# Convolution pieces, row-transform copies and transposes in another order in the tail of a four-layer kernel

## The chip, the cores and the metric

The program runs on one core of one Trainium2 chip. The metric is the device time of one execution in microseconds (us), lower is better. A core has engines with instruction queues of their own that run side by side and meet only at semaphores: TensorE (PE) multiplies matrices into the banks of PSUM (tile `ps`), VectorE (DVE), ScalarE (ACT) and GpSimd (POOL) do elementwise work, and SyncE (SP) starts transfers. Each queue is worked off in order, so an instruction that waits holds up all that stand behind it.

## What is computed

Eight images of 32 channels and 128 x 128 pixels go through four layers, each with a group normalisation ahead of it and a residual sum behind it:

```python
x = x + _L0_conv_ref(_gn(x), ...)   # 3x3 convolution, batch norm, relu, spectral curvature
x = x + _L1_conv_ref(_gn(x), ...)   # per-pixel 9x9 operator made of channel norms, then a mix
x = x + _L2_conv_ref(_gn(x), ...)   # gate made of the image's edges
x = x + _L3_conv_ref(_gn(x), ...)   # product of a spectral branch and a 3x3 convolution
return x
```

The change lies in the stage that computes layer 2 and the first part of layer 3. In the reference these are

```python
# layer 2
x_gray = jnp.mean(x, axis=1, keepdims=True)
dog = _conv(x_gray, gk1, pad) - _conv(x_gray, gk2, pad)
gx, gy = _conv(dog, sobel_x, 1), _conv(dog, sobel_y, 1)
mag = jnp.sqrt(gx * gx + gy * gy + 1e-06)
att = jax.nn.sigmoid(mag * gate_w[0] + gate_b[0])
return x * (1.0 + ALPHA * att)
# layer 3
g = _global_transform(c, w1, w2)    # rfft2, 16 x 16 modes mixed over channels, irfft2
l = _local_transform(c, conv_w, conv_b)   # 3x3 convolution with wrapped borders
return g * l
```

## The kernel before

The program has four stages, one after the other: layer 0's convolution over all images, the spectral part of layer 0 with the norms for layer 1, layer 1's operator (the longest), and the **tail**, in which layers 2 and 3 run as a pipeline over the images. Behind the tail come the mixing of the spectra for all images at once (`mix_spectrum`, L867), the last image's convolution, and a loop that transforms back, multiplies and stores.

The tail is written out by hand, with no scheduler: each engine has a loop over the period `t` (on DVE `i`), and the order of the calls in it is the order in its queue. Image rows lie on the partitions. In period `t` three images are under way:

- Image `t+1` in layer 2: ACT normalises it in 4 quarters of 8 channels (`normalise(gn2, ...)`, L936) into the tile `xn3[(t+1) % 2]`. PE sums its channels to a grey picture in four quarters (`gray_sum`, L811), then filters it (`blur` L772, `sobel` L778 and L780). ACT copies between these steps and makes the gate's factor in `mag_root` and `att_tanh` (L1106, L1114); DVE finishes it in `magnitude` and `attention` (L1529, L1534).
- Image `t` on its way from layer 2 to layer 3: DVE multiplies by the gate and adds (`attend`, L1516 and L1519), and takes the statistics for the next normalisation gn3 (L1226). PE forms the means and variances over partitions (`group_means` L574, `group_vars` L581), with DVE's `group_deviations`, `group_shift` (L1246) and `group_scale` (L1251, L1253) and ACT's `group_root` (L930) between them. ACT normalises with gn3 in four quarters. PE makes the row transforms (`dft_rows`, four per image, L789, in banks 6 and 7 in turn), ACT copies each of them out (`dft_out`, L1066), and PE makes the column transforms (`dft_columns`, L801). DVE transposes the normalised image into the layout of the convolution (`bands`, L1542 to L1544), and POOL adds the halo rows (L1215, L1216).
- Images `t-1` and `t-2` in the 3x3 convolution (`conv3`, L591): each image has two halves of nine taps, cut into three pieces of three taps. Half 0 of image `t-1` runs between the row transforms, half 1 of image `t-2` between the grey sums. ACT empties the banks 0 to 3 after each half (`conv3_out`, L1080).

Beside that POOL and DVE prepare image `t+2`: POOL adds layer 1's output (`tail_sum`, L1202), DVE takes its statistics for gn2, and the gn2 mean, variance and scale go through the same PE and DVE steps as those of gn3.

The waits that the prediction walks along are these. The row transform `n` waits for the copy `n-2` (same bank). The column transforms wait for all four copies. ACT's normalisation of image `t+1` waits for `gn2.ready` of that image, set by `group_scale`, and for the transposes of image `t-1`, since both images use the same tile:

```python
after(act, bands_ready, t)
after(act, dfth_mm, 4 * t)
for q in range(4):
    normalise(gn2, t + 1, q, xn3[(t + 1) % 2], xd[(t + 1) % 3])
```

The transposes wait for all gn3 normalisations of their image. `conv3` waits before its first tap until the banks are emptied; the pieces of half 1 need nothing new after that.

## Time and profile before

| | us |
|---|---|
| median of 3 runs | 3924.25 |
| lowest, highest | 3917.05, 3925.5 |
| the profiled execution's own time | 3922.26 |
| its span in the profile | 3920.1 |
| tail, about | 3185 to 3640 |
| mixing of the spectra | 3640 to 3717 |
| back transforms and output | 3745 to 3920 |

Engine busy time over the whole span: PE 3338.9 us (85%), DVE 2855.7 (73%), ACT 1849.5 (47%), POOL 2341.5 (60%). These shares come from layer 1's operator above all. A reader should look at the tail alone: the table by stretch gives each engine's busy time in it, and the timelines give the start and the busy time of each group of instructions, with the idle time ahead of it and what ended that in brackets. A wait in brackets that is marked "issue" is one for which the profile shows no releaser.

### The profile page before, as it was taken

The page shows a single profiled execution, that of the slowest core. Times are in us where ns is not written, and L with a number is a line of the kernel's source. Part 1 is how long each engine was busy: PE and PEld are TensorE (multiplying, and loading weights), DVE is VectorE, ACT ScalarE, POOL GpSimd, SP SyncE. Part 2 cuts the span into 40 slices and gives each one's busy share as a digit, 9 for nine tenths or more (in the row PEclk, how much of TensorE's full clock was granted, in tenths as well). Part 3 has the DMA queues.
Part 4 walks back from the last instruction along what each step waited for, and adds up shares of the span by engine and source line. Part 5 has one row for each costly group of instructions (what it writes and reads, how often), then busy time and mean ns, then how long its engine had stood idle before and what let it go on. Part 6 is the DMA issues. An engine that isn't in the chain of part 4 may idle for free.

```text
span 3920.1 us, 89862 instructions
## 1 busy us (share of the span) xinstructions
PE 3338.9 (85%) x32900; PEld 1184.0 (30%) x32900; DVE 2855.7 (73%) x3513; ACT 1849.5 (47%) x2702; POOL 2341.5 (60%) x1131
## 2 busy tenths in 40 slices
PE   4678999759999999999999999999999957787565
PEld 2343444312212212222222222222222245555454
DVE  3652544469989989989989989989999956655034
ACT  0114566355545545555555555555555455665011
POOL 0000000049999999999999999999999923321000
PEclk9899999879999999999999999999999967888665
DMA  6574898566656656666666666666666664535589
GB/s 158 120 167 99 164 196 169 124 164 155 154 133 148 153 139 145 158 141 144 150 149 143 145 152 147 141 149 151 141 149 159 141 152 118 154 101 128 140 191 251
DMA packets 495204, 586.47 MB, mean 150 GB/s; under 512 B 71970, under 2 KB 334754, under 8 KB 489435
## 3 DMA queue, kind: packets, MB, share of 16 engines
q1 hardware_dynamic: 484212, 563.65, 62.5%
q10 hardware_dynamic: 10560, 16.93, 1.8%
q8 instruction: 287, 4.70, 0.5%
q14 instruction: 145, 1.19, 0.1%
HBM read 409.91 MB, written 184.54 MB: 152 GB/s over the span
## 4 chain that ended last, share of the span: by engine, by line
PE 30%; POOL 29%; issue 28%; DVE 5%; ACT 4%; DMA 2%; SPq 1%; ACTq 0%; POOLq 0%; DVEq 0%
POOL arena L1183 27%; PE ps L591 8%; PE ps L632 7%; PE ps L639 4%; PE ps L703 3%; POOL arena L1171 2%; ACT arena L936 2%; PE ps L789 1%; PE ps L811 1%; DVE arena L1542 1%; PE ps L685 1%; PE ps L898 1%; PE ps L867 1%; DMA arena<-x_dram 1%; DMA w_conv<-in_conv_w 1%
## 5 line engine op out<-in xcount | busy, mean ns | idle before, releaser
L1183 POOL TENSOR_TENSOR arena<-arena 128x1024 f32<-128x1024 f32 x896 | 1931.0, 2196 | 556.2 <-ACT arena L1039 556.2
L1494 DVE TENSOR_TENSOR arena<-ps,arena 128x1024 f32<-128x1024 f32 x1792 | 2107.4, 1220 | 204.9 <-PE ps L685 174.3
L703 PE MATMUL ps<-arena,w_mix 128*32 128x512 f32 x10752 | 1438.5, 607 | 79.4 <-POOL arena L1183 79.4
L1039 ACT ACTIVATE arena<-ps 128x1024 f32<-128x1024 f32 x896 | 918.9, 1026 | 1026.3 <-PE ps L695 1015.3
L685 PE MATMUL ps<-arena,sel 48*128 48x512 bf16 x3584 | 702.5, 385 | 24.8 <-issue 16.1
L685 PEld LDWEIGHTS ps<-arena,sel 48*128 48x128 bf16 x3584 | 190.1, 93 | 945.5 <-issue 936.8
L591 PE MATMUL ps<-arena,w_conv 32*32 32x512 f32 x9216 | 354.0, 650 | 42.6 <-issue 34.3
L695 PE MATMUL ps<-norms,opw 57*128 57x512 bf16 x1792 | 348.1, 384 | 49.2 <-ACT arena L971 17.5
L703 PEld LDWEIGHTS ps<-arena,w_mix 128*32 128x32 f32 x10752 | 214.3, 108 | 467.5 <-issue 467.5
L936 ACT ACTIVATE arena<-arena,nmr,rstd 128x128 f32<-128x128 f32 x768 | 300.5, 481 | 33.0 <-DVE arena L1544 30.4
L632 PE MATMUL ps<-arena,circ 128*128 128x512 f32 x640 | 287.9, 595 | 14.1 <-ACT arena L950 14.1
L695 PEld LDWEIGHTS ps<-norms,opw 57*128 57x128 bf16 x1792 | 101.8, 93 | 435.3 <-issue 430.0
L591 PEld LDWEIGHTS ps<-arena,w_conv 32*32 32x32 f32 x9216 | 179.1, 107 | 178.8 <-issue 125.5
L1215 POOL COPY arena<-arena 32x130 f32<-32x130 f32 x32 | 33.8, 1057 | 327.7 <-DVE arena L1544 326.7
L1166 POOL TENSOR_TENSOR arena<-arena 128x1024 f32<-128x1024 f32 x62 | 133.0, 2145 | 95.7 <-ACT arena L980 95.7
L1580 DVE TENSOR_TENSOR arena<-arena,ps 128x512 f32<-128x512 f32 x64 | 43.7, 683 | 192.7 <-PE ps L898 163.3
L639 PE MATMUL ps<-arena,circ 128*128 128x512 f32 x384 | 176.3, 594 | 0.0
L632 PEld LDWEIGHTS ps<-arena,circ 128*128 128x128 f32 x640 | 120.3, 189 | 166.6 <-issue 166.6
L1226 DVE BATCH_NORM_STATS2 st<-arena 128x6 f32<-128x128 f32 x768 | 156.5, 278 | 7.1 <-POOL arena L1202 4.9
L1422 DVE TENSOR_TENSOR arena<-arena 128x512 f32<-128x512 f32 x64 | 44.3, 692 | 143.1 <-ACT arena L955 141.1
L1159 POOL TENSOR_TENSOR col<-col,powers 128x1 f32<-128x1 f32 x8 | 4.4, 549 | 241.1 <-DVE col L1282 241.1
L811 PE MATMUL ps<-arena,ident 128*128 128x128 f32 x512 | 78.8, 319 | 70.0 <-ACT arena L936 69.9
(151 smaller groups left out, 2195.2 us busy)
## 6 DMA issues: line engine op xcount, KB each, us to landing
arena<-pad SPq DMA_DIRECT2D x768, 260.0 KB, 7.7
split_dram<-arena SPq DMA_DIRECT2D x64, 768.0 KB, 3.6
arena<-split_dram SPq DMA_DIRECT2D x1536, 32.0 KB, 3.2
x_dram<-arena SPq DMA_DIRECT2D x16, 2048.0 KB, 7.8
l_dram<-arena SPq DMA_DIRECT2D x128, 256.0 KB, 4.2
arena<-l_dram SPq DMA_DIRECT2D x32, 1024.0 KB, 14.1
arena<-x_dram SPq DMA_DIRECT2D x16, 2048.0 KB, 16.4
pad<-arena SPq DMA_DIRECT2D x8, 2080.0 KB, 16.4
```

What stands on the lines that cost most here:

```text
L591: m = pe.matmul(ps[C * j:C * j + C, bank + g, :], weights[C * g:C * g + C, dy, dx, :], tile[C * g:C * g + C, r:r + CR, dx:dx + W], start=t ...
L632: m = pe.matmul(ps[:, n % 2, :], circ[:, d, :], yp[h % 2][:, 4 * n:4 * n + 4, 4 - d:4 - d + W], start=d == 0, stop=d == 4)
L639: m = pe.matmul(ps[:, 2 + n % 2, :], circ[:, 5 + d, :], yp[h % 2][:, 4 * n:4 * n + 4, 4 - d:4 - d + W], start=d == 0, stop=d == 2)
L685: m = pe.matmul(ps[:, 2 * (n % 2) + e, :], sel[ROWS2 * e:ROWS2 * e + SPLIT_ROWS, u % GROUP, :], split[ROWS2 * e:ROWS2 * e + SPLIT_ROWS, pa ...
L695: m = pe.matmul(ps[:, POOL_BANK + e, :], opw[ROWS2 * e:ROWS2 * e + KROWS, SPREAD[c], :], norms[ROWS2 * e:ROWS2 * e + KROWS, buf, half, :]. ...
L703: m = pe.matmul(ps[C * g:C * g + C, SUM + chunk % 2, :], w_mix[:, s, :], ring[:, (first + g // 2) % size, NPX * (g % 2):NPX * (g % 2) + NP ...
L936: m = nc.scalar.activation(tile[:, c, :], src[:, c, :], ACT.Identity, scale=rstd[:, gn.slot + n % 2, c:c + 1], bias=nmr[:, gn.slot + n % 2 ...
L1039: nc.scalar.activation(ring_p[:, slot, :], ps[:, POOL_BANK:POOL_BANK + 2, :].rearrange("p a n -> p (a n)"), ACT.Tanh).then_inc(tanh_p, 1)
L1166: nc.gpsimd.tensor_tensor(rest, tt, hml[:, 0, :], ALU.subtract).then_inc(rows_r, 1)
L1183: nc.gpsimd.tensor_tensor(slot, slot, pixels(chunk % 2, SPREAD[n // 2], n % 2), ALU.mult).then_inc(prod_p, 1)
L1226: m = nc.vector.bn_stats(st[:, c, :], tile[:, c, :])
L1494: nc.vector.tensor_tensor(slot, weights, pixels(par, ONCE[n // 2], n % 2), ALU.mult).then_inc(prod_d, 1)
```

## The change

In PE's loop of the tail the three pieces of the convolution's half 1 are placed otherwise: the first at the end of the period before, behind `dft_columns`, the second ahead of the first grey sum, the third ahead of the second grey sum. In ACT's loop each copy of a row transform comes one place later: copy 0 behind the third gn3 quarter, copy 1 behind the fourth, copy 2 behind the tanh. In DVE's loop `bands` goes ahead of `attention` and of `group_scale` of gn2. Nothing is added or removed; all loops of other stages are as before.

```diff
--- before.py
+++ after.py
@@ -827,10 +827,10 @@
             TAP_PARTS = ((0, 1, 2), (3, 4, 5), (6, 7, 8))
             for t in range(-2, B + 1):
                 for n in range(4):
+                    if t >= 2 and n < 2:
+                        conv3(t - 2, 1, TAP_PARTS[n + 1])
                     if 0 <= t + 1 < B:
                         gray_sum(t + 1, n)
-                    if t >= 2 and n < 3:
-                        conv3(t - 2, 1, TAP_PARTS[n])
                 if 0 <= t < B:
                     after(pe, dftw_copy, 3 * t)
                     group_means(gn3, t)
@@ -854,6 +854,8 @@
                     if t + 2 < B:
                         pe.wait_ge(gn2.shifted, t + 3)
                     dft_columns(t)
+                if 1 <= t < B:
+                    conv3(t - 1, 1, TAP_PARTS[0])
 
             def mix_spectrum():
 
@@ -1107,11 +1109,13 @@
                 for q in range(4):
                     if 0 <= t < B:
                         normalise(gn3, t, q, xn3[t % 2], xd[t % 3])
-                        if q:
-                            dft_out(t, q - 1)
+                        if q >= 2:
+                            dft_out(t, q - 2)
                 if 0 <= t + 1 < B:
                     act.wait_ge(mag_root, t + 2)
                     nc.scalar.activation(r2[:, :], rn[:, :], ACT.Tanh, scale=gate_h[:, 0:1], bias=gate_h[:, 1:2]).then_inc(att_tanh, 1)
+                if 0 <= t < B:
+                    dft_out(t, 2)
                 if t + 2 < B:
                     group_root(gn2, t + 2)
                 if 0 <= t < B:
@@ -1559,12 +1563,12 @@
                     tail_stats(i + 2)
                     group_deviations(gn2, i + 2, t)
                     group_shift(gn2, i + 2)
+                if i >= 0:
+                    bands(i)
                 if 0 < i + 1 < B:
                     attention(i + 1)
                 if i + 2 < B:
                     group_scale(gn2, i + 2, t)
-                if i >= 0:
-                    bands(i)
 
             for b in range(B):
                 x3, l3 = xe[b % 3], le[b % 3]
```

On PE, from the column transforms at the end of one period to the Sobel filter of the next; the rows of before:

```order
L801 MATMUL ps<-k,arena 32x32 x64
L811 MATMUL ps<-arena,ident 128x128 x8
L591 MATMUL ps<-arena,w_conv 32x512 x48
L811 MATMUL ps<-arena,ident 128x128 x8
L591 MATMUL ps<-arena,w_conv 32x512 x48
L811 MATMUL ps<-arena,ident 128x128 x8
L591 MATMUL ps<-arena,w_conv 32x512 x48
L811 MATMUL ps<-arena,ident 128x128 x8
L574 MATMUL ps<-st,k 128x32 x2
L772 MATMUL ps<-gray,k 128x128 x5
```

and the same place in the changed kernel:

```order
L801 MATMUL ps<-k,arena 32x32 x64
L591 MATMUL ps<-arena,w_conv 32x512 x96
L811 MATMUL ps<-arena,ident 128x128 x8
L591 MATMUL ps<-arena,w_conv 32x512 x48
L811 MATMUL ps<-arena,ident 128x128 x24
L574 MATMUL ps<-st,k 128x32 x2
L772 MATMUL ps<-gray,k 128x128 x5
```

Two pieces (96 matmuls) now stand between the column transforms and the first grey sum, one behind that sum, and the last three sums follow each other. (One matmul of the program shows as two in the profile's counts.)

On ACT, from the gn3 normalisations to the end of the period; before:

```order
L936 ACTIVATE arena<-arena,nmr,rstd 128x128 x16
L1066 COPY arena<-ps 128x512
L936 ACTIVATE arena<-arena,nmr,rstd 128x128 x8
L1066 COPY arena<-ps 128x512
L936 ACTIVATE arena<-arena,nmr,rstd 128x128 x8
L1066 COPY arena<-ps 128x512
L1114 ACT_TABLE_LOAD
L1114 ACTIVATE r<-rn,gate_h 128x128
L930 ACT_TABLE_LOAD
L930 ACTIVATE root<-sd 128x32
L1066 COPY arena<-ps 128x512
```

and in the changed kernel, whose line numbers are 2 higher here:

```order
L938 ACTIVATE arena<-arena,nmr,rstd 128x128 x24
L1068 COPY arena<-ps 128x512
L938 ACTIVATE arena<-arena,nmr,rstd 128x128 x8
L1068 COPY arena<-ps 128x512
L1116 ACT_TABLE_LOAD
L1116 ACTIVATE r<-rn,gate_h 128x128
L1068 COPY arena<-ps 128x512
L932 ACT_TABLE_LOAD
L932 ACTIVATE root<-sd 128x32
L1068 COPY arena<-ps 128x512
```

Three copies moved back by one place each; the two table loads stay.

On DVE, from `group_shift` to `attend`; before:

```order
L1246 TENSOR_SCALAR sd<-ps 128x32
L1534 TENSOR_SCALAR ra<-r 128x128
L1251 RECIPROCAL rstd<-root 128x32
L1253 SCALAR_TENSOR_TENSOR nmr<-mu,rstd 128x32
L1542 STREAM_TRANSPOSE arena<-arena 128x128x32
L1543 STREAM_TRANSPOSE arena<-arena 128x32
L1544 STREAM_TRANSPOSE arena<-arena 128x32
L1516 TENSOR_TENSOR arena<-arena,ra 128x1024 x4
```

and in the changed kernel, whose line numbers are 4 higher here:

```order
L1250 TENSOR_SCALAR sd<-ps 128x32
L1546 STREAM_TRANSPOSE arena<-arena 128x128x32
L1547 STREAM_TRANSPOSE arena<-arena 128x32
L1548 STREAM_TRANSPOSE arena<-arena 128x32
L1538 TENSOR_SCALAR ra<-r 128x128
L1255 RECIPROCAL rstd<-root 128x32
L1257 SCALAR_TENSOR_TENSOR nmr<-mu,rstd 128x32
L1520 TENSOR_TENSOR arena<-arena,ra 128x1024 x4
```

The three transposes moved ahead of the three small instructions, and stay behind `group_shift`.

## Rows read from the trace of the kernel before

**Rows 1.** Table by stretch: busy us (instructions) of each engine, PEclk, DMA share, GB/s.

```profile
3353.60:3414.60 61.00, 46.05 (x868) 31.40 (x868) 34.07 (x96) 36.40 (x85) 18.75 (x12) 0.86 0.52 140
3474.20:3531.70 57.50, 44.57 (x868) 31.17 (x868) 34.10 (x96) 36.40 (x85) 18.75 (x12) 0.86 0.25 75
```

**Rows 2.** Timeline of PE, period 5: start, busy us, instructions [idle before <- what ended it].

```profile
3477.43 3.78 PE L811 MATMUL ps<-arena,ident 128*128 128x128 f32 x16 [9.25 <-ACT arena L936]
...
3485.01 2.05 PE L811 MATMUL ps<-arena,ident 128*128 128x128 f32 x16
3486.99 3.41 PE L591 MATMUL ps<-arena,w_conv 32*32 32x512 f32 x96
...
3497.53 0.54 PE L574 MATMUL ps<-st,k 128*128 128x32 f32 x4
...
3523.58 2.12 PE L801 MATMUL ps<-k,arena 128*32 128x32 f32 x128 [1.89 <-issue]
```

**Rows 3.** Timeline of ACT, period 5.

```profile
3474.20 12.44 ACT L936 ACTIVATE arena<-arena,nmr,rstd 128x128 f32<-128x128 f32 x32 [5.07 <-DVE arena L1544]
3497.73 0.27 ACT L1092 COPY gray<-ps 128x128 f32<-128x128 f32 x1 [11.10 <-PE ps L811]
...
3503.28 6.26 ACT L936 ACTIVATE arena<-arena,nmr,rstd 128x128 f32<-128x128 f32 x16
3509.43 0.57 ACT L1066 COPY arena<-ps 128x512 f32<-128x512 f32 x1
...
3514.29 3.19 ACT L936 ACTIVATE arena<-arena,nmr,rstd 128x128 f32<-128x128 f32 x8
...
3523.38 2.13 ACT L1080 ACTIVATE arena<-ps,bias 128x1024 f32<-128x1024 f32 x2
...
3531.75 4.72 ACT L936 ACTIVATE arena<-arena,nmr,rstd 128x128 f32<-128x128 f32 x12 [5.11 <-DVE arena L1544]
```

**Rows 4.** Timeline of DVE, one row of period 1, then period 5.

```profile
3258.91 2.50 DVE L1235 TENSOR_TENSOR dev<-st,mu 128x32 f32<-128x32 f32 x2
...
3474.06 4.87 DVE L1516 TENSOR_TENSOR arena<-arena,ra 128x1024 f32<-128x1024 f32 x4
...
3483.78 6.27 DVE L1226 BATCH_NORM_STATS2 st<-arena 128x6 f32<-128x128 f32 x32
...
3523.04 0.35 DVE L1251 RECIPROCAL rstd<-root 128x32 f32<-128x32 f32 x1 [0.99 <-ACT root L930]
...
3523.53 8.05 DVE L1542 STREAM_TRANSPOSE arena<-arena 128x4096 f32<-128x4096 f32 x1
```

**Rows 5.** Timeline of PE, the means of period 1 and the first sum of period 6.

```profile
3258.04 0.61 PE L574 MATMUL ps<-st,k 128*128 128x32 f32 x4 [1.43 <-issue]
...
3534.99 3.78 PE L811 MATMUL ps<-arena,ident 128*128 128x128 f32 x16 [9.29 <-ACT arena L936]
```

**Rows 6.** Table by stretch, PE alone: PE busy, PEclk, DMA share, GB/s.

```profile
3504.00:3506.00 2.00, 0.95 (x31) 1.00 0.93 248
3524.00:3526.00 2.00, 1.70 (x116) 0.50 0.04 8
3262.00:3264.00 2.00, 1.90 (x9) 0.50 0.47 104
```

**Rows 7.** Timelines of DVE and PE, end of period 6 and period 7.

```profile
3579.42 8.10 DVE L1542 STREAM_TRANSPOSE arena<-arena 128x4096 f32<-128x4096 f32 x1
...
3581.82 10.64 PE L591 MATMUL ps<-arena,w_conv 32*32 32x512 f32 x288
3603.65 1.04 PE L574 MATMUL ps<-st,k 128*128 128x32 f32 x4 [11.19 <-issue]
...
3606.95 5.58 PE L591 MATMUL ps<-arena,w_conv 32*32 32x512 f32 x96
```

**Rows 8.** Timeline of PE: a piece in period 3, and the mixing of spectra.

```profile
3397.84 2.17 PE L591 MATMUL ps<-arena,w_conv 32*32 32x512 f32 x43 [2.04 <-issue]
...
3657.78 2.05 PE L867 MATMUL ps<-cs,arena 32*32 32x16 f32 x128 [7.45 <-issue]
```

**Rows 9.** DMA issues, 3180 to 3640 us: line, KB each, median us to landing.

```profile
arena<-x_dram SPq DMA_DIRECT2D x5, 2048.0 KB, 8.4
```

## Prediction

> **What bounds the kernel now.** I read first the table by stretch, then the timelines of PE, ACT and DVE over one period of the tail. The tail runs from about 3185 to 3640 us of the 3920.1 us span; nothing ahead of it or behind it is touched, so only its periods count. I call a period's start the moment when ACT begins the 32 gn2 normalisations of the next image: 3295.6, 3353.6, 3414.6, 3474.2 and 3531.75 for periods 2 to 6. So periods 2 to 5, four of one pattern, take 58.0, 61.0, 59.6 and 57.5 us; two of them stand in [rows 1]. No engine is full there: PE has 44.6 to 46.2 us of busy time, DVE 34.1, ACT 36.4, POOL 18.75. The period is a ring of waits, and it must be walked.
>
> Period 5, from 3474.20. ACT is done with its 32 normalisations after 12.44 us, then stands 11.10 us for PE's grey sum [rows 3]. DVE multiplies, adds and takes statistics and is done at 3490.05, but PE's means, which it waits for, start at 3497.53 [rows 2, 4]. Both wait for the same queue: PE starts the first grey sum 3.2 us into the period, and runs four sums with three convolution pieces between them, until 3497.7, 23.5 us in. PE's grey sum, with the convolution inside it, is what comes last. Then come means, blur, variances and Sobel, and ACT starts the gn3 normalisations at 3503.28: **29.1 us** after the period's start. From there: four quarters with three copies between them, tanh and its table, the root and its table (which waits for DVE's `group_shift`, and that for PE's variances; I read it at 3521.72), `attention`, `group_scale`, and only then the transposes at 3523.53. The next period starts 8.22 us later, at 3531.75: **28.5 us** after the start of the gn3 normalisations [rows 2 to 4].
>
> **Part 1, the convolution pieces.** At the clock's high level a quarter of the grey sum costs 1.98 us from its start to the next one's (3485.01 to 3486.99) and a piece 3.34 (3.41 less the same 0.07 of overlap) [rows 2]. After the change two of the three pieces stand ahead of the first sum, one of them behind the column transforms of the period before. I need that PE has room there: the column transforms end at 3525.7, and the next sum starts at 3534.99 after 9.29 us idle [rows 2, 5]. Two pieces are 6.7 us, so they fit. The first needs ACT to have emptied the banks (L1080, done at 3525.5, ahead of PE anyway [rows 3]), so that new wait costs nothing. At high clock the sums then end: first sum 3.2 to 5.2 us into the period, one piece to 8.5, second sum 10.5, third 12.5, fourth 14.5 (ACT's last quarter is there at 12.45). So PE comes down from 23.5 to 14.5. But the means wait for DVE too, which starts `attend` at the period's start and takes 16.0 us (3474.06 to 3490.05) [rows 4]; in the new order it starts 0.16 us ahead of ACT, which puts the means at 15.9. **What is late next is DVE's `attend`**, not PE, and of the 9.0 us only about 7.6 come through. From means to the first gn3 normalisation is 5.75 us now (3497.53 to 3503.28), less 0.3 since ACT's L1080 is over by the time the blur ends: 5.45. That gives 21.4 us instead of 29.1.
>
> The clock. After its 9.29 us of idle time PE's first sum takes 3.78 us instead of 2.05: it runs at 0.50, the low level (1.2 GHz), which the engine has had since the column transforms [rows 2, 6]. In the new order PE works until about 0.6 us into the period and then waits 2.6 us for ACT's first quarter. The gap of 1.89 us ahead of the column transforms brought it down; in 3504 to 3506, with 1.05 us idle, it stayed at 1.00 [rows 2, 6]. So I count a low spell here as likely. It can cost the 1.7 us of one sum; the fourth sum then ends at 16.2, just by DVE's 15.9. I add 0.5 us per period for it. By the same rows the gap before the means (14.5 to 15.9) may take the clock down in the periods where the first didn't.
>
> **Part 2, transposes ahead of `attention` and `group_scale`; copies later.** Moving the copies shifts ACT, not PE. A normalised quarter is 3.1 us and a copy 0.5 [rows 3]. The first copy comes 9.9 us after the start instead of 6.7, and the third row transform, which needs it, starts at 13.75 behind PE's pieces: 3.9 us of slack. The second copy ends at 13.7, wanted at 15.7: 2.0 us of slack. The quarters end at 13.0 instead of 14.2 (3514.29 + 3.19). The transposes wait for all four and then for `group_shift`, which PE's variances let go 18.5 us after the start; they stay where they are. So the transposes start at 18.55 instead of 20.25: 1.7 us earlier [rows 4]. `attention` and `group_scale` now stand behind them, and ACT's next normalisation needs their result: 0.14 for `attention`, 0.49 from the reciprocal to what follows `group_scale` (3523.04 to 3523.53), in all about 0.65 us more than now [rows 4]. Net **1.1 us**: 27.4 instead of 28.5. A new steady period is 21.4 + 27.4 + 0.5 = **49.3**, say 49.5 us.
>
> **Part 3, period 6 and 7.** Period 6 has no image of gn2 left, so no `group_shift` holds the transposes: they start as soon as ACT's last quarter is done, 13.0 us after 3561.07 instead of 18.35 (3579.42) [rows 7]. `attend` of the last image, and with it PE's wait of 11.19 us for the means at 3603.65 [rows 7], follow: 37.4 us after the gn3 start instead of 42.6, **5.2 us**, on top of the 7.7 of the front half. PE's pieces lie in that wait. Period 7 keeps its time: PE at a clock of 0.50 and then its three pieces lead there, and the copies have slack. The mixing of spectra and the output stage only shift.
>
> **Code fetch.** PE's gaps marked "issue" in the mixing of spectra come after every 128 matmuls; the 16 of them are 1.4 to 7.45 us, the long ones while many loads run; in period 3 such a gap of 2.04 us, and in period 4 a slow piece, lie in the second half [rows 8], and they are the reason why those periods are 3.5 and 2.1 us longer than period 5. The new order issues column transforms and two pieces on end; the same with three pieces stands in period 7 and takes 10.64 instead of 10.0 us [rows 7], so little is lost. In the second half the instructions stand as densely as before. Ends: none of these stalls left (0), or 2.04 us in each of the four periods and those of before (about 14). I take 3, half of what periods 2 to 4 show over period 5 (0.5 + 3.5 + 2.1). The Trainium skill (Runtime: NRT & Kernel Launch, section Instruction fetch mechanics) says that the next block of code is fetched while this one runs and that crossing a block is mostly hidden. By that rule this term would be 0 and the forecast 3 us lower; the gaps of [rows 8] speak against it.
>
> **The sum.** Period 0: 0.25 us (transposes earlier by 0.9, 0.65 more behind them). Period 1: 1.1 us; it has no convolution in its front half and keeps its 25 us there, which hold a DVE stall of 2.2 us [rows 4]. Periods 2 to 5: 236.2 us now, 4 x 49.5 + 3 = 201 after: 35.2. Period 6 to the means: 7.7 - 0.5 + 5.2 = 12.4. Together 49. The profiled execution took 3922.26 us for a span of 3920.10, the median of the runs is 3924.25; 49 us below the latter is **3875 us** (1.2%).
>
> **Transfers.** POOL adds the next image behind its halo copies, which follow the transposes, from about 9 us into the period, as now. Its x1 load goes out when the gn3 normalisations end, some 23 us ahead of that in the new period, and lands in 8.4 us in the tail (median) [rows 9]. So shorter periods still leave 14 us. SP's stores come no later than before in the period.
>
> **Rivals.**
> 1. *Low clock and stalls in every period.* In period 1, after a gap of 1.43 us before the means and a DVE stall, the clock was at 0.50 from 3262 on, and the front half took 25 us without any convolution [rows 4 to 6]. If each new period's gap before the means does that, blur, variances and Sobel, some 3.2 us of work, double but for what DVE and ACT do between: up to 2.7 us, five times, 13.5; with the stalls at 8 instead of 3 it is 18 us: about 3893.
> 2. *All stalls gone.* Pages of code fall otherwise, period 1 loses its 2.2 us stall, no low spells: 3 + 2.2 + 2.5 us less, 3867.
> 3. *Slower: the clock stays low.* PE's work is then 1.6 to 1.8 times as long: a sum took 3.78 us and, in period 7, a piece 5.58, against 2.05 and 3.41 [rows 2, 7]. Per period, with the row transforms at the sums' price, that is 6 x 2.2 + 8 x 1.7 = 27 us more than 41 us of work, 68 in all, and four to five periods become about 10 us longer than now: 3970. It decides when over a third of a period's work runs low. The clock of 1.00 in mid-period [rows 6] speaks against it, as PE will be idle less than now.
> 4. *No gain.* Pieces at the period's end hold the first sum back by as much as they free later. That needs over 6 us of new waiting there; the 9.29 us of idle speak against it. 3920 to 3928.
>
> **How the numbers follow.** The forecast, 3870 to 3884, 0.60. Rival 1 with what lies between, 3885 to 3900, 0.20. Rival 2, below 3870, 0.13. Rival 3, 0.04; rival 4, 0.03. Range 3864 to 3895: it leaves out rival 3 and the far ends of 1 and 2, some 0.15 in all. What a measurement can tell from no change is 0.2%, 8 us. Faster 0.93, same 0.03, slower 0.04.
>
> **What will show it.** ACT's first gn2 normalisations 49 to 50 us apart in periods 2 to 6; from there 21.5 us to the gn3 ones; PE's means right behind DVE's last statistics, no 8 us wait on DVE; the transposes right behind `group_shift`, in period 6 right behind the last quarter; PE's idle time before the first sum 2 to 3 us. I am wrong if the first sum starts later than 3.5 us into the period, if the means come later than 17 us into it, or if the row transforms wait for a copy.

## The result and the profile after

The changed kernel takes 3889.7 us (median of 4 runs, 3884.2 to 3892.5), the kernel before 3922.1 us in the runs beside it. The ratio is 0.9914, with a 95% interval from 0.9898 to 0.9930: 32.4 us faster, where the prediction had 49. Its profiled execution took 3892.5 us for a span of 3890.4 us.

The timelines of PE and ACT give the tail's periods. The table below is worked out from them for both kernels. "Means" is the time from the period's start to the start of PE's four means (L574), "to gn3" the time from there to ACT's first gn3 normalisation, "second half" the rest up to the next period's start (in period 6, up to the means of the last image).

```
                P0     P1     P2     P3     P4     P5     P6
means    before 15.30  15.97  23.81  23.81  22.46  23.33  23.57
         after  15.29  18.13  18.11  18.11  18.11  18.10  15.95
to gn3   before  5.41   9.08   5.74   5.74   5.75   5.75   5.75
         after   5.40   7.65   6.90   6.65   7.98   7.57   5.38
second   before 28.58  28.45  28.46  31.50  31.36  28.47  42.58
         after  27.76  27.45  27.47  30.47  29.89  28.96  37.39
period   before 49.29  53.50  58.01  61.05  59.57  57.55  71.90
         after  48.45  53.23  52.48  55.23  55.98  54.63  58.72
```

From the start of period 0 to the last means it is 410.9 us before and 378.7 after. So nearly all of the difference lies where the change was made: 0.8 us in period 0, 0.3 in period 1, 17.9 in periods 2 to 5, 13.2 in period 6. The stages around the tail shift the whole time as well, and by no pattern that an edit explains: over all kernels here the tail's period 0 begins between 3185.3 and 3201.6 us, and what follows the last means takes 309 to 322 us. For what an edit does in the tail, its trace is therefore the better witness, and for the whole the medians with their intervals.

The table by stretch shows one period of each length, and answers to [rows 1]: busy us (instructions) of PE, PEld, DVE, ACT and POOL, then PEclk, DMA share, GB/s.

```profile
3349.63:3404.86 55.23, 47.84 (x899) 33.56 (x891) 36.28 (x96) 36.53 (x85) 18.82 (x13) 0.91 0.58 154
3460.84:3515.47 54.63, 46.68 (x890) 33.66 (x868) 36.24 (x96) 36.41 (x85) 18.82 (x13) 0.88 0.27 79
```

DVE has 2.1 to 2.2 us more of busy time than in [rows 1] (36.28 against 34.07, 36.24 against 34.10), though the change gives it no new work. That is the first trace of what the prediction missed. The next three fences are the timelines of one period, in which the columns are start, busy us, engine, line, operation, tile, form, count, and in brackets the idle time before with what ended it. First PE from the end of period 4 through period 5, and then the means of the last image, which answers to [rows 2] and [rows 7]:

```profile
3454.91 7.49 PE L591 MATMUL ps<-arena,w_conv 32*32 32x512 f32 x192
...
3464.08 2.05 PE L811 MATMUL ps<-arena,ident 128*128 128x128 f32 x16 [1.69 <-ACT arena L938]
3466.07 3.40 PE L591 MATMUL ps<-arena,w_conv 32*32 32x512 f32 x96
3469.40 5.97 PE L811 MATMUL ps<-arena,ident 128*128 128x128 f32 x48
...
3478.94 1.03 PE L574 MATMUL ps<-st,k 128*128 128x32 f32 x4 [3.57 <-issue]
3479.78 2.48 PE L772 MATMUL ps<-gray,k 128*128 128x128 f32 x10
...
3489.73 2.45 PE L789 MATMUL ps<-k,arena 128*128 128x64 f32 x16 [1.55 <-ACT arena L938]
3492.11 4.49 PE L591 MATMUL ps<-arena,w_conv 32*32 32x512 f32 x96
...
3574.19 1.03 PE L574 MATMUL ps<-st,k 128*128 128x32 f32 x4 [4.56 <-issue]
```

The two pieces fit behind the column transforms, the first sum follows after 1.69 us at the clock's high level (2.05 us, not 3.78; it is 2.05 us in each of periods 2 to 5), and the fourth sum ends at 3475.4, 14.5 us into the period, as predicted. Then PE stands 3.57 us, not 1.4. Now ACT, which answers to [rows 3]:

```profile
3460.84 12.43 ACT L938 ACTIVATE arena<-arena,nmr,rstd 128x128 f32<-128x128 f32 x32 [4.88 <-DVE nmr L1257]
3475.41 0.27 ACT L1094 COPY gray<-ps 128x128 f32<-128x128 f32 x1 [2.14 <-PE ps L811]
...
3486.51 9.34 ACT L938 ACTIVATE arena<-arena,nmr,rstd 128x128 f32<-128x128 f32 x24
...
3515.47 12.45 ACT L938 ACTIVATE arena<-arena,nmr,rstd 128x128 f32<-128x128 f32 x32 [4.88 <-DVE nmr L1257]
```

ACT's wait for the grey sum is 2.14 us instead of 11.10, and its gn3 quarters stand in one group of 24. Now DVE, which answers to [rows 4], with the transposes of periods 5 and 6:

```profile
3460.64 5.02 DVE L1520 TENSOR_TENSOR arena<-arena,ra 128x1024 f32<-128x1024 f32 x4
3465.58 7.06 DVE L1523 TENSOR_TENSOR arena<-arena 128x1024 f32<-128x1024 f32 x4
...
3506.59 8.06 DVE L1546 STREAM_TRANSPOSE arena<-arena 128x4096 f32<-128x4096 f32 x1
...
3549.79 7.99 DVE L1546 STREAM_TRANSPOSE arena<-arena 128x4096 f32<-128x4096 f32 x1 [13.24 <-ACT arena L938]
```

The four adds of `attend` take 7.06 us, where the same four (L1519) took 5.00 us before. The transposes of period 6 no longer wait for a `group_shift` but for ACT, as the prediction said.

### The profile page after: what moved, and what is told of

Its sections match the earlier page's. It is cut to its first block, busy times and chain, and to the rows that moved or that the text cites. A ratio compares the mean times of both kernels' runs of the same rounds, so it can differ in the third digit from the quotient of the medians.

```text
span 3890.4 us, 89862 instructions
## 1 busy us (share of the span) xinstructions
PE 3348.1 (86%) x32900; PEld 1193.3 (31%) x32900; DVE 2864.0 (74%) x3513; ACT 1848.2 (48%) x2702; POOL 2340.5 (60%) x1131
## 3 DMA queue, kind: packets, MB, share of 16 engines
q14 instruction: 146, 1.19, 0.1%
## 4 chain that ended last, share of the span: by engine, by line
POOL 30%; PE 29%; issue 28%; DVE 5%; ACT 4%; DMA 2%; SPq 1%; ACTq 0%; POOLq 0%; DVEq 0%
POOL arena L1187 27%; PE ps L632 7%; PE ps L591 7%; PE ps L639 4%; PE ps L703 3%; ACT arena L938 2%; PE ps L789 2%; POOL arena L1175 2%; PE ps L685 1%; DVE arena L1546 1%; PE ps L900 1%; PE ps L869 1%; DMA arena<-x_dram 1%; DMA w_conv<-in_conv_w 1%; DVE arena L1584 1%
## 5 line engine op out<-in xcount | busy, mean ns | idle before, releaser
L685 PE MATMUL ps<-arena,sel 48*128 48x512 bf16 x3584 | 703.1, 386 | 25.2 <-issue 15.3
L591 PE MATMUL ps<-arena,w_conv 32*32 32x512 f32 x9216 | 357.7, 658 | 46.6 <-issue 38.5
L695 PE MATMUL ps<-norms,opw 57*128 57x512 bf16 x1792 | 348.7, 385 | 49.0 <-ACT arena L973 17.5
L1175 POOL TENSOR_TENSOR arena<-arena 128x1024 bf16<-128x1024 f32 x62 | 133.0, 2145 | 0.0
```

What stands on the lines that cost most here:

```text
L591: m = pe.matmul(ps[C * j:C * j + C, bank + g, :], weights[C * g:C * g + C, dy, dx, :], tile[C * g:C * g + C, r:r + CR, dx:dx + W], start=t ...
L685: m = pe.matmul(ps[:, 2 * (n % 2) + e, :], sel[ROWS2 * e:ROWS2 * e + SPLIT_ROWS, u % GROUP, :], split[ROWS2 * e:ROWS2 * e + SPLIT_ROWS, pa ...
L695: m = pe.matmul(ps[:, POOL_BANK + e, :], opw[ROWS2 * e:ROWS2 * e + KROWS, SPREAD[c], :], norms[ROWS2 * e:ROWS2 * e + KROWS, buf, half, :]. ...
L1175: nc.gpsimd.tensor_tensor(hml[:, 2, :], rest, hml[:, 1, :], ALU.subtract).then_inc(rows_l, 1)
```

## What made the adds longer: POOL beside DVE

POOL's timeline of the changed kernel in period 5 (copies of the halo, then the sums of the next image):

```profile
3460.28 0.28 POOL L1219 COPY arena<-arena 32x130 f32<-32x130 f32 x1 [36.77 <-DVE arena L1548]
...
3460.93 1.19 POOL L1219 COPY arena<-arena 32x130 f32<-32x130 f32 x1
...
3468.36 11.12 POOL L1206 TENSOR_TENSOR arena<-arena 128x1024 f32<-128x1024 f32 x4
```

And of the kernel before, DVE's adds and POOL's sums in a period:

```profile
3478.85 5.00 DVE L1519 TENSOR_TENSOR arena<-arena 128x1024 f32<-128x1024 f32 x4
...
3484.09 9.32 POOL L1202 TENSOR_TENSOR arena<-arena 128x1024 f32<-128x1024 f32 x4
```

Before, POOL's sums began 0.24 us behind the end of DVE's last add (3478.85 + 5.00 = 3483.85). In the new order `group_scale` stands behind the transposes, so POOL's copies, which the transposes release, get a short start on DVE: two begin before `attend` does (3460.28 and 3460.61 against 3460.64) and run 0.28 us each, and only the later ones take 1.19 us beside it. POOL is therefore through its copies in the middle of DVE's adds, and its first sum begins at 3468.36. The group of adds by line, with shortest, median and longest in ns, has one long one:

```profile
L1523 DVE TENSOR_TENSOR arena<-arena x32: 1208/1307/3379, 3199.9 to 3566.6; 128x1024 f32<-128x1024 f32 x32
```

An add of 1.31 us has become one of 3.38, longer by 2.07 us, about the length of one of POOL's sums (9.3 us for four), and POOL's four sums take 11.12 us instead of 9.32. Neither engine shows idle time for it: the wait lies inside the busy time of the instruction. DVE's statistics, which read one tensor, don't meet POOL in this way: in the kernel before they took 6.27 us from 3483.78 on [rows 4], right beside POOL's sums of 9.32 us.

The Trainium skill states such a rule (SBUF — State Buffer, section SBUF: two separate sides): DVE and GpSimd share a pair of ports, and whichever of a DVE operation with two SBUF inputs and a GpSimd operation that reads SBUF starts first "gets the pair for the whole instruction", while the other is fully blocked. The trace agrees, in 1.31 against 3.38 us for the add and 0.28 against 1.19 us for the copy. The prediction did not weigh it.

This gives a theory and rivals to it. **Theory:** the 2.15 us in every period from 1 to 5 come from POOL's sums beside DVE's adds; what then is still above 5.4 us between means and gn3 is the clock, which falls in the gap before the means. **Against it:** that transfers slow the adds; that the collision costs nothing and the clock alone makes the front halves long; and, for the second halves of periods 3 to 5, that code fetch makes them long, as the prediction held.

## Experiments

All ratios are to the kernel before, timed beside each in the same batch. Times of stretches are from each kernel's profiled execution, in the measure of the table above.

**POOL's sums behind the adds.** One wait on POOL, ahead of `tail_sum(t + 2)`:

```
                 after(pool, halo_ready, t)
                 if t + 2 < B:
+                    pool.wait_ge(x3_done, 4 * (t + 1))
                     tail_sum(t + 2)
```

> The changed kernel with one more wait: POOL starts the four sums of the image after next (L1206) only when DVE's four adds of attend (L1523) are over. Theory: in periods 1 to 5 one DVE add took 3.4 us instead of 1.3 and POOL's four sums 11.12 instead of 9.32 because the two engines use the same way to the memory in turn; the sums began 1.3 us before the adds' middle, where before the change they began 0.24 us after the last add. Then DVE's attend takes 16.0 us in every period instead of 18.1, the means come 16.0 us into the period, and the gap ahead of them is 1.4 instead of 3.56 us, so the clock falls in fewer periods: 5 x 2.15 = 11 us for the former and up to 6 for the latter, 3872 to 3880 us. Rival, a code fetch stall of DVE that happens to fall into the adds: the adds stay at 7.1 us for four, the time stays at 3889 or gets longer.

Measured: 3880.1 us, 0.9887 [0.9869, 0.9904]. The means start 15.92 to 15.95 us into periods 1 to 6, instead of 18.1: the collision with the adds is gone, and with it 2.15 us. But the stretch from means to gn3 is now 7.9 to 9.0 us in periods 1 to 5. DVE's, POOL's and PE's rows of period 3 show why:

```profile
3366.40 2.42 DVE L1240 TENSOR_TENSOR dev<-st,mu 128x32 f32<-128x32 f32 x2
...
3359.36 9.28 POOL L1206 TENSOR_TENSOR arena<-arena 128x1024 f32<-128x1024 f32 x4 [2.35 <-issue]
...
3365.53 0.61 PE L574 MATMUL ps<-st,k 128*128 128x32 f32 x4 [1.40 <-issue]
...
3369.50 1.06 PE L581 MATMUL ps<-dev,k 128*128 128x32 f32 x4 [2.18 <-DVE dev L1245]
```

POOL's sums end at 3368.64, and two of DVE's small deviation operations, 0.2 us each elsewhere, take 2.42 us together and end at 3368.82. It is the same collision at another place, and PE stands 2.18 us for it. Period 0, which had no collision before, now has one and takes 8.98 us there instead of 5.40. So the period gains only a part of the 2.15 us, and the interval overlaps that of the changed kernel.

**Keeping PE busy ahead of the means.** The changed kernel with 14 small matmuls into a free bank ahead of `group_means`:

```
+                    if 0 <= t + 1 < B:
+                        for c in range(14):
+                            pe.matmul(ps[:, 4, 64:64 + W], ident[:, :], xn3[(t + 1) % 2][:, c, :], start=True, stop=True)
                     group_means(gn3, t)
```

> The changed kernel with 14 more matmuls (28 by the profile's count, 3.5 us) between the last grey sum and the means, written to an unused place in bank 4. They fill PE's gap of 3.56 us and change nothing that is computed. Theory: the gap takes the granted clock down, and blur, variances and Sobel after it then run at 0.50; with the gap filled the clock stays at 1.00 and the stretch from the means to the first gn3 normalisation is 5.4 us in all periods instead of 6.65 to 7.98. In periods 2 to 5 that is 1.5 + 1.2 + 2.5 + 2.1 = 7 us, in period 1 about 2; in period 6 the gap is only 1.4 us, so the means come 2 us later there. Together 3882 us. Rival, the stretch is longer for another reason, such as code fetch: 3889 or 3891.

Measured: 3878.6 us, 0.9895 [0.9876, 0.9915]. From means to gn3 every period now takes 5.3 to 5.6 us, instead of 6.65 to 7.98; the means start at 17.5 to 18.75 us. PE's rows there:

```profile
3414.77 3.29 PE L838 MATMUL ps<-arena,ident 128*128 128x128 f32 x28
3417.89 0.54 PE L574 MATMUL ps<-st,k 128*128 128x32 f32 x4
3418.26 1.36 PE L772 MATMUL ps<-gray,k 128*128 128x128 f32 x10
```

The blur takes 1.36 us, where it took 2.48 in the row of 3479.78 above, and the means 0.54 instead of 1.03. So the 1.2 to 2.6 us above 5.4 are the clock, which in the changed kernel falls to 1.2 GHz in each of periods 1 to 5, in the gap or within 1.8 us behind it. The work is the same. What each of the two causes is worth in the whole time can't be read from these two runs, since the first moves the collision instead of removing it. The interval overlaps that of the changed kernel, as in the first experiment.

**Both together,** with 6 small matmuls instead of 14:

> Both together, with 6 more matmuls (1.5 us) for the then shorter gap of 1.4 us. Theory: means at 16.0 us, 5.4 us from there to the first gn3 normalisation in all periods 1 to 6, so 21.4 us of front half as forecast; what is then left over the forecast lies in the second halves (code fetch, 7 us over 27.4 each). 3869 to 3874 us. Rival for the clock: the same time as with POOL's wait alone, within 1 us.

Measured: 3879.5 us, 0.9889 [0.9871, 0.9907], no different from either alone, and 5.5 us above what was expected: a miss. By the time alone this is what the rival said (within 1 us of POOL's wait alone, 3880.1). The trace shows why that doesn't rule out the clock. Periods 1 to 5 have means at 15.9 to 17.0 us and 6.5 to 9.0 us to gn3: the filler itself puts the means 1 us later in periods 2 to 4, and the deviations still collide with POOL's sums (the longest of them takes 1.4 to 2.3 us instead of 0.2), against which filler doesn't help.

**PE's part alone.** The kernel before with the diff's two hunks on PE and nothing else:

```
+                    if t >= 2 and n < 2:
+                        conv3(t - 2, 1, TAP_PARTS[n + 1])
...
-                    if t >= 2 and n < 3:
-                        conv3(t - 2, 1, TAP_PARTS[n])
...
+                if 1 <= t < B:
+                    conv3(t - 1, 1, TAP_PARTS[0])
```

> The kernel before with the PE part of the change alone (the three convolution pieces moved); copies and transposes stand as before. Theory: attend follows the transposes at once here, so POOL's halo copies stand beside DVE's multiplications as before and its sums begin just after DVE's adds; the adds take 5.0 us for four, the means come 16.0 us into the period instead of 23.5, and the second half stays 28.5 us or more with its fetch gaps. Periods 2 to 5 about 50.5 us and more, gain 4 x 7.4 + 7.6 = 37 less 3 for the clock: 3888, as fast as the whole change or faster. Rival, without the collision theory: the whole change is faster by what its second part brings (11 us), and this one takes about 3900.

Measured: 3890.8 us, 0.9926 [0.9910, 0.9942], 30.2 us less than before, so within the intervals as much as the whole change. The adds are short here (4.7 to 5.0 us for four), as expected, and the means come at 15.3 to 16.0 us. But the collision is not gone: POOL's sums meet DVE's deviations in every one of periods 1 to 5, and from means to gn3 it is 8.2 to 11.3 us. All deviations of this kernel, and period 4, where both are hit and a POOL copy waits through all of `attend`:

```profile
L1237 DVE TENSOR_TENSOR dev<-st,mu x28: 195/208/2412, 3213.3 to 3584.7; 128x32 f32<-128x32 f32 x28
```

```profile
3408.33 9.05 POOL L1217 COPY arena<-arena 32x130 f32<-32x130 f32 x1 [34.37 <-DVE arena L1546]
...
3424.39 4.71 DVE L1237 TENSOR_TENSOR dev<-st,mu 128x32 f32<-128x32 f32 x2
```

**Everything but PE's part.** The changed kernel with those hunks undone:

> The changed kernel with PE in the order of before, so the transposes and the copies alone. Forecast of this part: 1.1 us a period and 5.2 us in period 6, 12 us in all. The collision of POOL's sums with DVE's adds is there too (adds 7.1 us), but PE's grey sum, ready 23.5 us into the period, hides it in periods 2 to 6; only period 1 pays 2 us. Theory: 10 us below before, 3911, all of it in second halves (27.4 instead of 28.5; 37.4 instead of 42.6). Rival, if the part is worth nothing: 3921.

Measured: 3908.0 us, 0.9962 [0.9947, 0.9976], 16.4 us less. By the medians the parts alone give 30.2 + 16.4 = 46.6 us and together 32.4, each with some 6 us of uncertainty. In the tail, by the traces, they give 24.7 + 11.7 = 36.4 us and together 32.2 (the trace of PE's part is of an execution of 3901.1 us, one of two of its six that were 10 us above the others). So the parts give less together than added up, but by how much, 4 or 14 us, is open. With the rest alone the means come at 22.7 to 24.4 us in periods 2 to 6, behind PE's sums, and the longer adds (3.39 us) are hidden. With PE's part they would show, but there the deviations had cost about as much: from the start of the periods 1 to 5 to their gn3 normalisations it is 125.8 us in all with PE's part alone and 127.3 with the whole change. The collision had only moved, from the deviations to the adds.

**POOL's sums behind the magnitudes,** so that neither adds nor deviations meet them:

```
                 if t + 2 < B:
+                    pool.wait_ge(mag_sum, t + 2)
                     tail_sum(t + 2)
```

> The changed kernel, but POOL starts its four sums only behind DVE's magnitude, some 21 us into the period, so that they stand beside no DVE instruction that reads two tiles, neither attend's adds nor the deviations of gn3. Theory: the same collision that cost attend 2.15 us in the changed kernel costs the deviations (first one 2.4 us instead of 0.2) with POOL's first wait, and cost them 2.5 us in period 1 of the kernel before; it, and the gap of 2.2 us ahead of PE's variances that it makes, is why the stretch from the means to the gn3 normalisations grew to 7.9 to 9.0 us there. Then means at 15.95 us and 5.4 to 6.5 us behind them in periods 1 to 5 (against 7.9 to 9.0): 10 to 15 us below the kernel with the first wait, 3865 to 3870. Rival, the stretch is long only because of the clock: it stays at 7.5 us or more, 3878 to 3880. What speaks for a loss: the sums and the l1 loads behind them come later, and the gn2 statistics need the sums by 37 us.

Measured: 3868.4 us, 0.9857 [0.9842, 0.9873]. From means to gn3 it is 5.4 us in periods 0, 1, 2, 5 and 6, and 5.75 in 3 and 4. The deviations by line, in the first experiment and in this one:

```profile
L1240 DVE TENSOR_TENSOR dev<-st,mu x28: 195/203/2317, 3208.8 to 3567.8; 128x32 f32<-128x32 f32 x28
```

```profile
L1240 DVE TENSOR_TENSOR dev<-st,mu x28: 196/206/214, 3205.3 to 3551.9; 128x32 f32<-128x32 f32 x28
```

The longest is 0.214 us instead of 2.317. No load of the tail was taken away, though those that wait for the sums come later with them; the kernel without these loads, below, settles it. What changed is where POOL's sums stand. The second halves are 28.8 to 29.0 us in four of the periods, against 27.4. In periods 3 and 4 the means are late by 2.7 and 1.1 us. The interval is clear of that of the changed kernel. The tail is 361.4 us, where the forecast (49 us off 410.9) amounts to 361.9; in part that is luck, since the late means and the second halves of 29 us are not in the forecast.

**The halo copies behind `attend`, too:**

```
                 pool.wait_ge(bands_ready, t + 1)
+                pool.wait_ge(x3_done, min(4 * (t + 2), 4 * B))
                 for g in range(G):
```

> As the one with late sums, and POOL's halo copies too wait until attend's adds are over (some 9 us into the period). Theory: beside the copies DVE's four multiplications take 5.0 us and the adds 4.9, alone 4.62 each (period 0 shows it), and a POOL copy 1.19 instead of 0.29 us; so attend is 0.7 us shorter in every period from 1 to 6 and the means come 15.25 us in. The gap before them shrinks to 0.7 us, and the clock falls seldom. 4 to 8 us below the kernel with late sums alone, about 3860. Rival, DVE isn't held by the copies: no difference beyond 1 us.

Measured: 3862.6 us, 0.9841 [0.9827, 0.9855]. DVE's multiplications and adds, and POOL's copies behind them with the sums later still:

```profile
3286.51 4.62 DVE L1522 TENSOR_TENSOR arena<-arena,ra 128x1024 f32<-128x1024 f32 x4
3291.05 4.62 DVE L1525 TENSOR_TENSOR arena<-arena 128x1024 f32<-128x1024 f32 x4
...
3295.83 0.29 POOL L1221 COPY arena<-arena 32x130 f32<-32x130 f32 x1 [30.34 <-DVE arena L1525]
...
3309.18 9.32 POOL L1206 TENSOR_TENSOR arena<-arena 128x1024 f32<-128x1024 f32 x4 [10.75 <-issue]
```

Even the copies cost DVE 0.4 us in each group of four: 4.62 against 5.0. The means come at 15.3 us where nothing else delays them, 0.65 us earlier than in the experiment ahead of this. In periods 2 and 3 they are at 16.8 and 19.6, as late ones stood in periods 3 and 4 there, and the second halves of 1 and 3 to 5 are 29.0 to 30.4. The interval overlaps that of the experiment ahead of this.

**Loads as the cause of the long second halves.** The changed kernel without the tail's layer-1 loads of images 3 to 7; POOL then adds what its tile held before, so the result is another:

> The changed kernel without the loads of layer 1's output for images 3 to 7 (10 of 2 x 1 MB; POOL adds a tile that is not refilled, so the result is another). They run from 20 to 36 us of a period, just over PE's second half. Theory: PE's waits in the second half (30.5, 29.9 and 29.0 us in periods 3 to 5 against 27.45 in periods 1 and 2) are fetches of code that these loads delay; without them all second halves take 27.4 to 27.6 us, 7 us less together, and the time is about 3882. Rival, they come from elsewhere (stores, or places in the code): the second halves stay spread from 27.4 to 30.5 us.

Measured: 3888.8 us (two runs), 0.9914 [0.9895, 0.9932], no different from the changed kernel and 7 us above what was expected. Its adds, beside POOL's sums and without the loads:

```profile
L1520 DVE TENSOR_TENSOR arena<-arena x32: 1211/1306/3387, 3201.2 to 3565.1; 128x1024 f32<-128x1024 f32 x32
```

In periods 2 to 5 one add still takes 3.38 us and the means still come at 18.1. So these loads aren't what slows DVE. The second halves of periods 3 to 5 are 28.99 to 29.01 instead of 30.47, 29.89 and 28.96: a rest of 1.6 us over 27.4 stays without any of these loads. Whether the loads carry the 1.5 and 0.9 us that periods 3 and 4 lost, one trace doesn't show. Its PE rows in period 3:

```profile
3378.93 2.43 PE L786 MATMUL ps<-k,arena 128*128 128x64 f32 x16 [1.55 <-ACT arena L935]
3381.29 4.52 PE L588 MATMUL ps<-arena,w_conv 32*32 32x512 f32 x96
```

The row transform takes 2.43 us and the piece 4.52, as at 3489.73 in the changed kernel. Both stand behind a gap of 1.55 us. The clock of the changed kernel in period 2 and the second half of period 3 (PE alone: PE busy, PEclk, DMA share, GB/s):

```profile
3313.00:3315.00 2.00, 0.00 (x0) 1.00 0.70 295
...
3318.00:3320.00 2.00, 2.00 (x10) 0.50 0.97 249
...
3379.00:3381.00 2.00, 2.00 (x24) 0.50 1.19 199
```

The first is the gap ahead of the means of period 2, the second the Sobel filter behind them, the third the row transform behind the gap of period 3. In the gap the clock is still at 1.00; in both places behind a gap it is at 0.50, that is 1.2 GHz. So the theory for the second halves changed: not code fetch but the clock, and filler ahead of the row transform should take the excess away.

**Filler ahead of the means and of the first row transform,** on the kernel with late copies and sums:

```
+            def fill(n, bank=4):
+                for c in range(n):
+                    pe.matmul(ps[:, bank, 64:64 + W], ident[:, :], circ[:, c % 8, :], start=True, stop=True)
...
+                    fill(3)
                     group_means(gn3, t)
...
+                        if n == 0:
+                            fill(6, 7)
                         dft_rows(t, n)
```

> The kernel with all of POOL's work late, and matmuls that nobody reads in two of PE's gaps: 3 of them (0.75 us) ahead of the means, 6 (1.5 us) in the gap of 1.55 us ahead of the first row transform. Theory: what is left over 27.4 us in the second halves (0 to 3 us a period) is mainly the clock, which falls to 0.50 behind that gap in some periods (a row transform of 2.45 to 2.94 and a piece of 4.5 to 5.5 us instead of 2.0 and 3.4). Filled, the second halves of periods 1 to 5 take 27.4 to 27.8 us, 3 to 6 us less in all: 3857 to 3860. Rival, the rest is fetching of code: the pieces stay slow in these periods, and the time stays at 3862 or gets up to 2 us longer by the matmuls added.

Measured: 3857.2 us (3853.4 to 3868.1), 0.9822 [0.9804, 0.9840], the fastest here, 68 us less than before; the interval overlaps that of the kernel without filler. (Its trace is of the slowest of its executions, 3868.1 us, in which 322 us lie behind the last means.) The second halves are 27.41 to 27.45 us in all of periods 1 to 5: the excess of up to 3 us is gone. PE's rows there:

```profile
3310.05 1.60 PE L827 MATMUL ps<-circ,ident 128*128 128x128 f32 x12
3311.68 2.00 PE L789 MATMUL ps<-k,arena 128*128 128x64 f32 x16
3313.61 3.41 PE L591 MATMUL ps<-arena,w_conv 32*32 32x512 f32 x96
```

The row transform takes 2.00 us instead of 2.45 and the piece 3.41 instead of 4.49. The filler adds matmuls to the stream and removes none, so code fetch had no reason to become better. This decides for the clock in these second halves. In the changed kernel it accounts for 3.0 us in period 3 (row transform 2.94 instead of 2.00, piece 5.47 instead of 3.41) and 1.5 in period 5. Period 4 is mixed, by this row at a granted clock of 1.00:

```profile
3440.05 1.90 PE L591 MATMUL ps<-arena,w_conv 32*32 32x512 f32 x35 [0.23 <-issue]
```

At the pace of a whole piece (3.41 us for 96) these 35 take 1.24 us. With the gap that is 0.9 of its 2.5 us which isn't the clock. Such a stall exists in the kernel with filler too, elsewhere. In period 4 the means are at 17.9, with this row in the burst of column transforms and pieces:

```profile
3386.31 4.84 PE L591 MATMUL ps<-arena,w_conv 32*32 32x512 f32 x93 [2.53 <-issue]
```

It stands 2.53 us for nothing that the trace shows, at a place where no input seems to be missing.

**Filler ahead of the first grey sum as well:**

```
+                        if n == 0 and t >= 1:
+                            for _ in range(3):
+                                pe.matmul(ps[:, 7, :], ident[:, :], circ[:, 0:4, :], start=True, stop=True)
```

> The kernel with POOL late and two gaps filled, and the third gap filled too: 3 matmuls over 512 columns (some 2.6 us at the high clock) between the two early convolution pieces and the first grey sum of a period. Theory: with the first sum at 1.00 in every period the fourth sum ends at 14.5 us and the means come at 15.3 us in all periods, where they came at 16.0 to 17.9 us in periods 2 to 5 without it: about 6 us less, 3851 to 3854. Rival: the means came late there through code fetch, since column transforms and pieces stand on end (one gap of 2.53 us marked issue stood ahead of a piece in period 4); then some periods stay at 17 us or later, and with the work added the time is 3857 to 3860.

Measured: 3869.4 us, 0.9864 [0.9841, 0.9886]. A miss: 15 to 18 us above what was expected of it. The second halves stay at 27.4 to 27.5 us, but the means of periods 2 to 5 come at 18.9 to 19.5 us, instead of 16.0 to 17.9. PE's rows around one of the bursts:

```profile
3432.84 4.23 PE L591 MATMUL ps<-arena,w_conv 32*32 32x512 f32 x80
...
3438.43 4.32 PE L591 MATMUL ps<-arena,w_conv 32*32 32x512 f32 x112 [1.36 <-issue]
3442.68 2.84 PE L839 MATMUL ps<-circ,ident 128*128 128x512 f32 x6
...
3456.71 0.54 PE L574 MATMUL ps<-st,k 128*128 128x32 f32 x4
```

The burst has gaps that "issue" ended, and it is so late that with the filler, 2.84 us, the first sum starts 8.1 us into the period instead of 3.2 and the sums no longer end ahead of DVE. So the rival, stalls in the burst, was right about the means (later than 17 us), and the filler made it worse. Filler costs its own time as soon as PE has no slack.

**The copies as before,** the rest changed:

```
-                        if q >= 2:
-                            dft_out(t, q - 2)
+                        if q:
+                            dft_out(t, q - 1)
...
-                if 0 <= t < B:
-                    dft_out(t, 2)
```

> The changed kernel with ACT's copies of the row transforms where they were before. Theory: in periods 0 to 5 the transposes wait for group_shift, so the copies bring nothing; only in period 6 do the transposes start 1.2 us later. 3890 to 3892 us beside 3890 for the whole change. Rival, the copies matter in every period through the order on ACT: 5 us or more.

Measured: 3891.7 us, 0.9921 [0.9902, 0.9941], no different from the changed kernel within the intervals. Period 6 shows the term by itself: 38.77 us instead of 37.39 from gn3 to the last means, as the last quarter comes later and the transposes wait for it there. The other periods' second halves are 27.43 to 27.48 in three cases, as with the late copies, since `group_shift` sets the transposes there; that agrees with "they stay where they are".

**POOL's two waits on the kernel before,** without the change:

> The kernel before with POOL's copies and sums late, as in the fastest version. Theory: the collision cost the kernel before only in period 1 (2.2 us in the deviations, and up to 1.5 us by the clock), and attend's 0.7 us is hidden behind PE's grey sums in periods 2 to 5 but not in 6: 3 to 5 us, 3917 to 3920. So the collision was harmless there and became a cost of the change. Rival: POOL's place is worth as much there as in the changed kernel, 27 us: 3895.

Measured: 3907.6 us, 0.9953 [0.9935, 0.9971], 17.7 us less, where 3917 to 3920 was expected: a miss. In the tail it gains 8.6 us (402.3 instead of 410.9 from period 0 to the last means): 3.7 from means to gn3 in period 1, where the collision with the deviations is gone, 0.7 from its earlier means, 2.9 in period 3 and 1.5 in period 4, whose second halves are 28.5 and 28.4 us instead of 31.5 and 31.4. The 4.4 us of period 1 are what the theory said; those of 3 and 4 come from the low clock and the stall of the kernel before, which stand elsewhere here (period 2 has a second half of 30.0). The stretch behind the last means, which the two waits don't touch, was 5 us shorter in its profiled execution (311.2 against 316.5 us). The same stretch lies between 309 and 322 us in the other kernels, without a pattern that follows an edit. What sets it is open; differences of 5 us between these kernels aren't to be read as effects of the tail.

For all kernels, the tail from period 0 to the last means, by the traces, in us:

```
before 410.9   before_pool_late 402.3   all_but_pe 399.2   pe_only 386.2
after 378.7    copies_back 378.6        no_l1_loads 376.0
pool_waits_fill 374.2   pool_waits 373.7   fill_gap 368.6
pool_late 363.6   fill_all 361.5   sums_late 361.4   pool_late_fill 353.0
```

## Why the prediction was right, and where its sum was off

The sign and the range were right, 3889.7 in 3864 to 3895; the forecast of 3875 was 15 us too low. The measured time lies in the band 3885 to 3900, to which the prediction gave 0.20, and not in its own 3870 to 3884 with 0.60; that it is inside the range is owed to the room left for rival 1. One of its own signs of being wrong came true: the means come 18.1 us into periods 1 to 5, where 17 was the limit. And the periods 2 to 5 are 52.5 to 56.0 us, not 49 to 50. Its picture of the ring of waits held wherever nothing else came in. Point by point:

**Which wait comes last (Part 1), right.** The pieces fit, the new wait for L1080 cost nothing, and DVE's `attend` is next. In period 6, where POOL has no more sums, the means come at 15.95 us (predicted 15.9), the gn3 normalisations 5.38 later (5.45), the last means 37.39 later (37.4). The predicted 21.4 us stand there as 21.3.

**The step that failed: "the means wait for DVE too, which [...] takes 16.0 us".** It took the length of `attend` from the order before, where POOL's sums started 0.24 us behind the last add. The change moves `group_scale` behind the transposes that release POOL, and the prediction said of POOL only that it adds the next image "from about 9 us into the period, as now". The two engines then meet. That is 2.15 us in each of periods 1 to 5; in 2 to 5 it takes 8.6 us of the expected 35.2. The experiments with POOL's waits show it: 15.95 instead of 18.11 us. The collision also cost more than its own length, as the next point says.

**The clock, mis-sized.** The text named the gap before the means, but priced all low spells at 0.5 us per period, from one sum. The first sum in fact ran high (2.05 us in each of periods 2 to 5). The spell came at the means, where the collision had made the gap 3.57 us, and cost 1.2 to 2.6 us in each of periods 2 to 5, some 5.3 us beyond the allowance. Rival 1 had this mechanism, with "up to 2.7 us", and its time of 3893 was nearer than the forecast. What it lacked was the reason that makes the gap long: where the gap stayed at 1.4 us and no deviation was hit (period 6 here, periods 1, 2 and 5 with late sums), means to gn3 took 5.38 to 5.42 us.

**Period 1, misread.** The prediction called the 2.50 us of [rows 4] a DVE stall and let it stay or go by chance. It was the collision of the deviations with POOL's sums, in the kernel before as well. Its POOL row, whose sums end at 3261.25, with DVE released at 3261.41:

```profile
3251.98 9.27 POOL L1202 TENSOR_TENSOR arena<-arena 128x1024 f32<-128x1024 f32 x4
```

With POOL later the same stretch takes 5.38 to 5.41 us instead of 9.08. In the changed kernel it is traded for the collision with the adds: means 2.16 us later, gn3 1.43 us sooner behind them, so the period gained 0.3 us instead of 1.1.

**Part 2, right where the clock stayed up.** The second halves of periods 1 and 2 are 27.45 and 27.47 us (predicted 27.4).

**"Code fetch", wrong in its cause for most of it.** It allowed 3 us for four periods. The second halves of 3 to 5 had 7.1 us over 27.4. Filler ahead of the row transform takes all of it away. By the rows of the changed kernel the low clock behind the gap of 1.35 to 1.55 us makes up about 6.2 of it, and 0.9 us in period 4 are a stall. In the kernel before, the two signs that were read as one cause were two: in period 4 the clock was low, in period 3 it was not (PE alone, as in [rows 6]).

```profile
3396.00:3398.00 2.00, 0.16 (x16) 1.00 0.30 60
...
3448.00:3450.00 2.00, 2.00 (x44) 0.53 1.20 195
```

So the 2.04 us of [rows 8] stay a stall without a clock drop, and the slow piece of period 4 was the clock. By the rule of the Trainium skill (Runtime: NRT & Kernel Launch, section Instruction fetch mechanics), crossing a block of code is mostly hidden; the gaps in the burst, 2.53 us in one kernel and 1.36 us in another, speak against this, as [rows 8] did. That these gaps are code fetch is argued, not shown: they are ended by "issue" at places where all inputs are there.

**Part 3, right:** 13.2 us gained in period 6, against 12.4.

The sum for periods 2 to 5: predicted 201 with its allowances (4 x 49.25 + 3 = 200, rounded up by 1), measured 218.3. The 18.3 us above 200 are 8.8 at the means (8.6 collision), 5.3 from means to gn3, 4.2 in the second halves. With the 0.8 us that period 1 gained less, and 1.4 that periods 0 and 6 gained more, that is the whole difference between 49 and the 32 us of the tail.

## What to carry to other kernels

When a change moves an engine's release, look at what that engine then runs beside, and not only at whether it still comes in time: with DVE reading two tensors while POOL works, a duration read from a trace holds only for the overlap in which it was read. An operation that is longer than its sisters without idle time before it (1.3 against 3.4 us, 0.2 against 2.3) is a sign of a wait on the other engine, and one more semaphore wait that moves POOL's work into a part of the period where DVE has none of it can give more than it costs (here a ratio of 0.9857 instead of 0.9914). After a reorder that leaves an engine waiting, look at PE's clock behind each new gap, and price it by the length of the work behind the gap on the ring, not by one instruction group.

## What the hardware did that was not expected

- Adds and sums of 128x1024 on DVE and POOL don't share: an add of 1.31 us took 3.38 beside a sum, a copy on POOL 1.19 instead of 0.28, and an operation on 128x32 elements 2.32 instead of 0.2 us. The add and the small operation lost about the same, 2.1 us, close to one sum (2.33 us): what counted was the length of the operation ahead, not of the one that waited. Once, with PE's part alone, a copy took 9.05 us, through DVE's eight operations on end.
- A gap of only 1.55 us among small matmuls was followed by the clock's low level in some periods and not in others (second halves of 27.47 and 30.47 us with the same instructions). Six more small matmuls in that gap, with three ahead of the means and POOL's work late, made periods 1 to 5 alike (27.41 to 27.45).
- Filler is no free gain: ahead of the first sum it turned 3857 into 3869 us, in a queue that was already late.
